# The attention mask moved from VectorE to GpSimd, the value copies from ScalarE to VectorE, and a layer norm folded into two fused operations

## The chip, the cores and the metric

The kernel runs on one core of a Trainium2 chip. The metric is the device time of one launch in microseconds. Before the change it took 445.38 us (median of three runs, 444.36 to 445.75).

The engines are named as in the profile: PE is TensorE (matrix products and transposes), DVE is VectorE, ACT is ScalarE, POOL is GpSimd, SP is SyncE, which here only issues DMAs. Each engine works through its own instruction queue in order and waits for the others by semaphores. SBUF is the on-chip memory, PSUM holds PE's results in eight banks.

## The reference, cut to what matters

Sixteen frames of 128 tokens by 128 channels pass through two decoder layers: cross attention to 120 context tokens with a feed-forward part, then a second cross attention with relative positions and another feed-forward part. The change touches the second attention and the layer norm behind it:

```python
attn = einsum('bidn,bjdn->bijn', hq, hk)                    # content scores, 16 heads
attn = attn + take_along_axis(b_full, idx, axis=2)          # relative position scores, shifted per row
attn = attn + ...                                           # the ub and vb terms
attn = attn / sqrt(128)
attn = where(attn_mask[..., None], -INF, attn)              # mask: 128 x 120 per frame, one for all heads
attn = softmax(attn, axis=2)
out  = einsum('bijn,bjdn->bidn', attn, hv)                  # hv: values of the context, 120 x 64 a head
out  = out * sigmoid(q @ head_w)
out  = out.reshape(...) @ Wo + residual
out  = (out - mean) / sqrt(var + 1e-5) * ln_g + ln_b
```

The result of this norm is added to the running frame x. In the inputs the mask is all false, but it is read and applied.

## The kernel before, in words

Everything is fp32. There are three stages, each a software pipeline over frames: the first attention (to about 126 us), the first feed-forward part (to about 170 us), and a third stage, `layer1(s, par)`, that does the second attention and its feed-forward part together. The change is only in the third stage.

In step s of the third stage different frames t are at different depths: frame s has its queries, keys and position products made, frame s-1 its content scores, frame s-2 its maxima and exponentials, frame s-3 and s-4 their scaling, transposes, value products and output, frame s-4 its norm, frames s-5 to s-7 the quantised feed-forward part. The order on every engine is written out by hand in `layer1`; buffers come in pairs, chosen by `p`. The 16 heads stand in four groups of four; group g of `prob[p]` is 128 x 480 (4 heads x 120 keys). The first steps, with few frames in flight, are the ramp here, the last ones, with no new frames, the drain. Steps 10 and 11 form a loop that runs once; all others are unrolled.

The relative shift is done through DRAM. PE makes unshifted position products; ACT copies them to `relw` (L567 to L627); SP stores them to `rel_scratch` and loads them back with a row stride one short (`store`, `shifted`, L255 to L266) into `relr[p]`. Half 1 (groups 2 and 3, semaphore `relr1`) is loaded at the end of step t, half 0 (groups 0 and 1, `relr0`) at the start of step t+1. DVE adds the content scores from PSUM to `relr` and writes `prob` (L1017, L1019, L1023 and, in the next step, L862; semaphores `added2`, `added3`, `added1`, `added0`). Each such addition also frees a PSUM bank that PE waits for.

Before the change DVE then applied the mask to each sum: `cap` is 0 where masked and 3e38 elsewhere, and `min(cap - 1e9, sum)` is taken, four operations of 128 x 480 a frame (L886, L897, L905, L1044; semaphore `masked`). The maxima (L874, L967, L969, L988) waited for `masked`. ACT takes the exponentials with their sums (L530), DVE the reciprocals (`rsum`, L1039 and L914), and POOL multiplies the probabilities by them (`scale_probs`, L383: groups 1 and 0 after the first `rsum` of the step, groups 3 and 2 after the second). PE transposes the scaled probabilities in two blocks (`probs_transpose`, L1262: first groups 0 and 1, then 2 and 3), ACT copies them out (`probT`), PE multiplies them with `hv`.

The values `hv` come from two PE products of 120 x 512, and ACT copied both from PSUM to SBUF (L563 and L602; `hv1` and `hv0` free the banks 0 and 6).

The norm of frame s-4: DVE takes mean and variance of `uo`, POOL the reciprocal root (L409), DVE `(uo - mean) * rstd` (L998), POOL multiplies by `ln_g` (L411), waits behind a spacer (L413) and adds `xb` = x + `ln_b` into `x_all` (L415; semaphore `x_done`, for which DVE's statistics of the next norm wait at L854).

## Time and profile before

The profiled execution took 446.94 us, its span (first to last instruction) 445.1 us; the rest lies around the span.

| engine | busy us | share of the span | instructions |
|---|---|---|---|
| PE, products | 413.2 | 93% | 6147 |
| PE, weight loads (beside the products) | 313.6 | 70% | 6147 |
| DVE | 374.7 | 84% | 1230 |
| ACT | 376.3 | 85% | 1478 |
| POOL | 250.2 | 56% | 364 |

The mean granted TensorE clock was 0.982 of full speed. Busy shares are means over all stages. The chain of work that ended last lies for 74% on PE, 12% on DVE, 6% on ACT. A column "idle before" in a view is the time in which the engine stood before an instruction, with the engine and line that ended the wait.

### The profile page before, as it was taken

The page shows a single profiled execution, that of the slowest core. Times are in us where ns is not written, and L with a number is a line of the kernel's source. Part 1 is how long each engine was busy: PE and PEld are TensorE (multiplying, and loading weights), DVE is VectorE, ACT ScalarE, POOL GpSimd, SP SyncE. Part 2 cuts the span into 40 slices and gives each one's busy share as a digit, 9 for nine tenths or more (in the row PEclk, how much of TensorE's full clock was granted, in tenths as well). Part 3 has the DMA queues.
Part 4 walks back from the last instruction along what each step waited for, and adds up shares of the span by engine and source line. Part 5 has one row for each costly group of instructions (what it writes and reads, how often), then busy time and mean ns, then how long its engine had stood idle before and what let it go on. Part 6 is the DMA issues. An engine that isn't in the chain of part 4 may idle for free.

```text
span 445.1 us, 16726 instructions
## 1 busy us (share of the span) xinstructions
PE 413.2 (93%) x6147; PEld 313.6 (70%) x6147; DVE 374.7 (84%) x1230; ACT 376.3 (85%) x1478; POOL 250.2 (56%) x364
## 2 busy tenths in 40 slices
PE   7999999999789997999999999999999999998782
PEld 6555565555456776877888888887878878887570
DVE  5799999989768884597788889888889978989865
ACT  1899999998955555599999999999999999999861
POOL 4297888878866651023346345554644654456654
PEclk9999999999989999999999999999999999999887
DMA  7251000000000002998766668567657856854000
GB/s 204 72 183 38 15 9 11 11 8 9 7 1 2 0 2 50 263 217 206 149 153 148 143 152 196 127 154 156 148 133 158 190 134 131 192 136 88 7 7 24
DMA packets 54392, 44.88 MB, mean 101 GB/s; under 512 B 43952, under 2 KB 49328, under 8 KB 54320
## 3 DMA queue, kind: packets, MB, share of 16 engines
q1 hardware_dynamic: 53616, 43.59, 40.9%
q8 instruction: 46, 0.75, 0.7%
q10 hardware_dynamic: 704, 0.32, 0.3%
q14 instruction: 26, 0.21, 0.2%
HBM read 22.92 MB, written 20.97 MB: 99 GB/s over the span
## 4 chain that ended last, share of the span: by engine, by line
PE 74%; DVE 12%; ACT 6%; POOL 2%; issue 2%; DMA 1%; SPq 1%; POOLq 0%; ACTq 0%; DVEq 0%
PE PS L1052 64%; PE PS L1262 4%; PE PS L1068 3%; ACT prob L530 2%; PE PS L1228 1%; DMA wr<-in_wr 1%; DVE nmax L715 1%; DVE nmax L717 1%; DVE relr L763 1%; POOL prob L326 1%; DVE relw L758 1%; DVE nmax L686 1%; PE PS L1218 1%; DVE probT L693 1%; DVE nmax L780 1%
## 5 line engine op out<-in xcount | busy, mean ns | idle before, releaser
L383 POOL TENSOR_TENSOR prob<-prob,rsum 128x480 f32<-128x480 f32 x63 | 65.4, 1059 | 88.7 <-DVE rsum L914 61.4
L530 ACT ACTIVATE prob<-prob,nmax 128x120 f32<-128x120 f32 x256 | 100.5, 426 | 0.0
L446 ACT ACTIVATE prob<-PS,nmax 128x120 f32<-128x120 f32 x256 | 89.6, 394 | 4.2 <-DVE nmax L780 2.5
L326 POOL TENSOR_TENSOR prob<-prob,rsum 128x480 f32<-128x480 f32 x64 | 62.5, 987 | 23.8 <-DVE rsum L753 12.7
L446 ACT ACTIVATION_READ_ACCUMULATOR prob<-PS,nmax 128x1 f32 x256 | 61.5, 240 | 0.0
L530 ACT ACTIVATION_READ_ACCUMULATOR prob<-prob,nmax 128x1 f32 x256 | 59.2, 231 | 0.0
L1052 PE MATMUL PS<-xnT,wq 128*128 128x128 f32 x288 | 43.1, 286 | 2.2 <-ACT xnT L599 1.1
L1052 PE MATMUL PS<-probT,hv 120*64 120x128 f32 x512 | 36.4, 286 | 5.3 <-ACT probT L617 3.2
L1052 PE MATMUL PS<-ctx,wk 128*128 128x120 f32 x288 | 41.1, 279 | 0.0
L1052 PE MATMUL PS<-rT,qv 64*32 64x152 f32 x2048 | 40.8, 292 | 0.3 <-DVE qu L881 0.3
L1052 PEld LDWEIGHTS PS<-probT,hv 120*64 120x64 f32 x512 | 28.4, 140 | 17.5 <-issue 7.7
L1052 PEld LDWEIGHTS PS<-xnT,wq 128*128 128x128 f32 x288 | 35.9, 191 | 5.2 <-issue 1.4
L1052 PE MATMUL PS<-wv,ctx 128*120 128x512 f32 (+1 forms) x96 | 39.1, 489 | 0.0
L1052 PE MATMUL PS<-wo,oT_pairs 128*128 128x128 f32 x256 | 36.2, 286 | 0.0
L1052 PEld LDWEIGHTS PS<-ctx,wk 128*128 128x128 f32 x288 | 36.0, 192 | 0.2 <-issue 0.2
L1052 PE MATMUL PS<-kT,qu 64*128 64x120 f32 x512 | 32.7, 276 | 2.3 <-issue 1.5
L1052 PE MATMUL PS<-relw,qT 32*128 32x480 f32 x128 | 34.4, 613 | 0.4 <-DVE relw L758 0.4
L1052 PEld LDWEIGHTS PS<-rT,qv 64*32 64x32 f32 x2048 | 31.0, 105 | 5.4 <-issue 4.0
L1052 PEld LDWEIGHTS PS<-wo,oT_pairs 128*128 128x128 f32 x256 | 31.8, 195 | 4.1 <-issue 4.0
L1052 PEld LDWEIGHTS PS<-kT,qu 64*128 64x128 f32 x512 | 30.3, 188 | 3.2 <-issue 1.8
L1068 PEld LDWEIGHTS PS<-ident,prob 64*120 64x120 f32 x512 | 18.1, 137 | 19.1 <-issue 19.1
L1068 PE MATMUL PS<-ident,prob 64*120 64x64 f32 x512 | 22.3, 228 | 5.4 <-POOL prob L326 2.9
(197 smaller groups left out, 1073.8 us busy)
## 6 DMA issues: line engine op xcount, KB each, us to landing
rel_scratch<-relw SPq DMA_DIRECT2D x128, 152.0 KB, 2.6
relr<-rel_scratch SPq DMA_DIRECT2D x64, 240.0 KB, 4.5
ctx<-in_ctxT SPq DMA_DIRECT2D x32, 60.0 KB, 1.9
out_x<-fin SPq DMA_DIRECT2D x16, 64.0 KB, 4.0
x_all<-in_x SPq DMA_DIRECT2D x1, 640.0 KB, 7.8
wr<-in_wr SPq DMA_DIRECT2D x1, 512.0 KB, 6.3
wq<-in_wq SPq DMA_DIRECT2D x1, 512.0 KB, 3.6
wk<-in_wk SPq DMA_DIRECT2D x1, 512.0 KB, 4.4
```

What stands on the lines that cost most here:

```text
L326: return pool.tensor_tensor(pr, pr, cols(rsum[p], g, HG).unsqueeze(2).to_broadcast([S, HG, SK]), ALU.mult)
L383: return pool.tensor_tensor(pr, pr, cols(rsum[p], g, HG).unsqueeze(2).to_broadcast([S, HG, SK]), ALU.mult)
L446: last = act.activation(cols(prob[p], n, SK), cols(scores, q, SK), ACT.Exp, bias=nmax[p][:, n:n + 1], accum_out=ssum[p][:, n:n + 1])
L530: last = act.activation(cols(pr, n, SK), cols(pr, n, SK), ACT.Exp, bias=bias[:, n:n + 1], accum_out=total[:, n:n + 1])
L686: dve.tensor_reduce(out=cols(nmax[p], 2, HG), in_=heads(PS[:, 3, 0:HG * SK], HG), op=ALU.max, axis=AX.X, negate=True).then_inc(A0["nmax"], 1)
L693: dve.tensor_copy(query_half(probT0[0], 1), heads(PS[0:SK, 6, :], 2 * HG)).then_inc(A0["probT1"], 1)
L715: dve.tensor_reduce(out=cols(nmax[p], 0, HG), in_=heads(PS[:, 0, 0:HG * SK], HG), op=ALU.max, axis=AX.X, negate=True).then_inc(A0["nmax"], 1)
L717: dve.tensor_reduce(out=cols(nmax[p], 1, HG), in_=heads(PS[:, 2, 0:HG * SK], HG), op=ALU.max, axis=AX.X, negate=True).then_inc(A0["nmax"], 1)
L758: dve.tensor_tensor(heads(kexp[p], HG), PS[:, 4, S:S + SK].unsqueeze(1).to_broadcast([D, HG, SK]), kmask_sb[:, :].unsqueeze(2).to_broadcas ...
L1052: return pe.matmul(o, a, b, start=start, stop=stop)
L1068: last = pe.transpose(PS[0:SK, bank, q * S // 2:(q + 1) * S // 2], cols(prob[p], g * HG + q, SK)[rows], ident_sb[rows, rows])
L1262: last = pe.transpose(PS[0:SK, bank, q * S // 2:(q + 1) * S // 2], cols(prob[p], g * HG + q, SK)[rows], ident_sb[rows, rows])
```

## The change

The four mask operations on DVE are gone. `cap` is now the mask times -1e30 (one operation as before, but at the start of DVE's step), and POOL adds it to the four groups of the reloaded position scores in `relr`, in place, before DVE adds the content scores. DVE's additions therefore wait for `masked` (two groups, then four) where they waited for `relr1` and `relr0`, and the maxima wait for the additions. On POOL the four additions stand between the two pairs of scalings. Both value copies move from ACT to DVE: `hv1` behind `qu0`, `hv0` behind the quantising. The norm becomes `(uo - mean) * ln_g` and `uo * rstd + xb`, two fused operations on DVE; POOL keeps the reciprocal root.

```diff
-BIG = 3.0e38
+NEG_MASK = -1.0e30
 ...
# POOL, layer1
+                def mask_scores(p, g):
+                    r = heads(cols(relr[p], g, HG * SK), HG)
+                    return pool.tensor_tensor(r, r, cap[p][:, :].unsqueeze(1).to_broadcast([S, HG, SK]), ALU.add)
                 t, p = s - 3, 1 - par
                 if on(t):
                     pool.wait_ge(A1["rsum"], 2 * t + 1)
                     scale_probs(p, 1).then_inc(A1["scaled1"], 1)
                     scale_probs(p, 0).then_inc(A1["scaled0"], 1)
+                t, p = s - 1, 1 - par
+                if on(t):
+                    pool.wait_ge(A1["cap"], t + 1)
+                    pool.wait_ge(A1[f"relr1{p}"], 2 * loads(t, p))
+                    mask_scores(p, 2).then_inc(A1["masked"], 1)
+                    mask_scores(p, 3).then_inc(A1["masked"], 1)
+                    pool.wait_ge(A1[f"relr0{p}"], 2 * loads(t, p))
+                    mask_scores(p, 1).then_inc(A1["masked"], 1)
+                    mask_scores(p, 0).then_inc(A1["masked"], 1)
+                t, p = s - 3, 1 - par
+                if on(t):
                     pool.wait_ge(A1["rsum"], 2 * t + 2)
                     scale_probs(p, 3).then_inc(A1["scaled3"], 1)
 ...
-                    pool.wait_ge(A1["onorm"], t + 1)
-                    pool.tensor_tensor(uo[p][:, :], uo[p][:, :], g_sb[:, :], ALU.mult).then_inc(A1["og"], 1)
-                    pool.wait_ge(A1["og"], t + 1)
-                    pool.tensor_tensor(gap_p[:, :], mhalf[:, :], mhalf[:, :], ALU.add)
-                    xt = x_all[:, bass.ds(t, 1), :].rearrange("p a d -> p (a d)")
-                    pool.tensor_tensor(xt, xb[p][:, :], uo[p][:, :], ALU.add).then_inc(A1["x_done"], 1)
# ACT, layer1
-                    act.wait_ge(A1["hv_ps"], 2 * t + 1)
-                    after(act, A1["av"], 4 * t - 4)
-                    act.activation(cols(hv[p], 1, 512), PS[0:SK, 0, :], ACT.Copy).then_inc(A1["hv1"], 1)
 ...
-                    act.activation(cols(hv[p], 0, 512), PS[0:SK, 6, :], ACT.Copy).then_inc(A1["hv0"], 1)
# DVE, layer1, at the start of the step
+                t, p = s - 1, 1 - par
+                if on(t):
+                    dve.wait_ge(A1[f"mask_loaded{p}"], loads(t, p))
+                    dve.tensor_scalar(cap[p][:, :], mask_sb[p][:, :], NEG_MASK, None, ALU.mult).then_inc(A1["cap"], 1)
 ...
-                    dve.wait_ge(A1["masked"], 4 * t + 1)
+                    dve.wait_ge(A1["added1"], t + 1)
 ...
-                    sc = heads(cols(prob[p], 3, HG * SK), HG)
-                    dve.scalar_tensor_tensor(out=sc, in0=cap[p][:, :].unsqueeze(1).to_broadcast([S, HG, SK]), scalar=NEG, in1=sc,
-                                             op0=ALU.add, op1=ALU.min).then_inc(A1["masked"], 1)
 ...
+                    dve.wait_ge(A1["hv_ps"], 2 * t + 1)
+                    after(dve, A1["av"], 4 * t - 4)
+                    dve.tensor_copy(cols(hv[p], 1, 512), PS[0:SK, 0, :]).then_inc(A1["hv1"], 1)
 ...
+                t, p = s - 2, par
+                if on(t):
+                    dve.wait_ge(A1["hv_ps"], 2 * t + 2)
+                    dve.tensor_copy(cols(hv[p], 0, 512), PS[0:SK, 6, :]).then_inc(A1["hv0"], 1)
 ...
                     dve.tensor_scalar(ve2[p][:, :], mv2[p][:, 1:2], 1e-5, None, ALU.add).then_inc(A1["ovar"], 1)
+                    dve.scalar_tensor_tensor(out=uo[p][:, :], in0=uo[p][:, :], scalar=mv2[p][:, 0:1], in1=g_sb[:, :],
+                                             op0=ALU.subtract, op1=ALU.mult).then_inc(A1["og"], 1)
 ...
-                    dve.tensor_scalar(uo[p][:, :], uo[p][:, :], mv2[p][:, 0:1], rstd2[p][:, :], ALU.subtract, ALU.mult)\
-                       .then_inc(A1["onorm"], 1)
+                    dve.wait_ge(A1["og"], t + 1)
+                    dve.wait_ge(A1["xb"], t + 1)
+                    dve.scalar_tensor_tensor(out=row(x_all, t), in0=uo[p][:, :], scalar=rstd2[p][:, :], in1=xb[p][:, :],
+                                             op0=ALU.mult, op1=ALU.add).then_inc(A1["x_done"], 1)
 ...
-                    dve.wait_ge(A1[f"relr1{p}"], 2 * loads(t, p))
+                    dve.wait_ge(A1["masked"], 4 * t + 2)
 ...
-                    dve.wait_ge(A1[f"relr0{p}"], 2 * loads(t, p))
+                    dve.wait_ge(A1["masked"], 4 * t + 4)
```

In the changed program POOL's queue at the ramp, up to step 3, reads as follows (before, then now). `rstd` is the reciprocal root for the norm of frame s+2, for which DVE's `xn` waits; `prob<-prob,rsum` are the scalings, `relr<-relr,cap` the mask additions.

```order
L419 TENSOR_TENSOR rstd<-ve,mhalf 128x1 x4
L425 TENSOR_TENSOR xb<-x_all,ln_b 128x128
L383 TENSOR_TENSOR prob<-prob,rsum 128x480 x4
L419 TENSOR_TENSOR rstd<-ve,mhalf 128x1
L425 TENSOR_TENSOR xb<-x_all,ln_b 128x128
```

```order
L428 TENSOR_TENSOR rstd<-ve,mhalf 128x1 x2
L387 TENSOR_TENSOR relr<-relr,cap 128x480 x4
L428 TENSOR_TENSOR rstd<-ve,mhalf 128x1
L387 TENSOR_TENSOR relr<-relr,cap 128x480 x4
L428 TENSOR_TENSOR rstd<-ve,mhalf 128x1
L434 TENSOR_TENSOR xb<-x_all,ln_b 128x128
L383 TENSOR_TENSOR prob<-prob,rsum 128x480 x2
L387 TENSOR_TENSOR relr<-relr,cap 128x480 x4
L383 TENSOR_TENSOR prob<-prob,rsum 128x480 x2
```

Four mask additions now stand ahead of `rstd` in steps 1 and 2, and between the pairs of scalings from step 3 on.

On DVE the same place, step 2 (frame 0 at its maxima), from `xn` at the end of step 1 to the second copy of the keys; `qu` are the query halves, `nmax` the maxima.

```order
L1031 TENSOR_SCALAR xn<-x_all,mv,rstd 128x128
L1044 SCALAR_TENSOR_TENSOR prob<-cap,prob 128x480
L862 TENSOR_TENSOR prob<-PS,relr 128x480
L869 TENSOR_SCALAR qu<-PS,ub 128x512
L874 TENSOR_REDUCE nmax<-prob 128x4
L881 TENSOR_SCALAR qu<-PS,ub 128x512
L886 SCALAR_TENSOR_TENSOR prob<-cap,prob 128x480
L892 TENSOR_SCALAR cap<-mask 128x120
L897 SCALAR_TENSOR_TENSOR prob<-cap,prob 128x480
L901 COPY xn_all<-xn 128x128
L905 SCALAR_TENSOR_TENSOR prob<-cap,prob 128x480
L952 COPY kT<-PS 128x480
```

```order
L1028 TENSOR_SCALAR xn<-x_all,mv,rstd 128x128
L864 TENSOR_SCALAR cap<-mask 128x120
L867 TENSOR_TENSOR prob<-PS,relr 128x480
L874 TENSOR_SCALAR qu<-PS,ub 128x512
L879 TENSOR_REDUCE nmax<-prob 128x4
L886 TENSOR_SCALAR qu<-PS,ub 128x512
L892 COPY hv<-PS 120x512
L895 COPY xn_all<-xn 128x128
L941 COPY hv<-PS 120x512
L945 COPY kT<-PS 128x480
```

The four mask operations have left, `cap` stands ahead of the last score addition, and the two value copies have come in, one directly behind the second `qu` and one ahead of the copy of the keys.

## Rows read from the trace of the kernel before

**Rows 1.** Busy time by stretch (start:end us, length; each engine; granted clock, DMA, GB/s).
```profile
260.00:400.00 140.00, 138.44 (x2513) 115.95 (x2511) 123.71 (x363) 135.16 (x489) 71.85 (x123) 1.00 0.66 152
120.00:128.00 8.00, 5.92 (x72) 3.91 (x72) 5.46 (x20) 5.69 (x20) 7.42 (x8) 0.79 0.01 3
```
**Rows 2.** Timeline of PE (start us, us, line, operation, count, idle before).
```profile
191.96 0.27 PE L1350 MATMUL PS<-ident,xn 128*128 128x128 f32 x1
...
208.08 0.69 PE L1262 MATMUL PS<-ident,prob 64*120 64x64 f32 x16
...
317.45 0.69 PE L1262 MATMUL PS<-ident,prob 64*120 64x64 f32 x16
...
321.78 1.06 PE L1052 MATMUL PS<-xnT,wq 128*128 128x128 f32 x8
...
407.67 1.09 PE L1052 MATMUL PS<-probT,hv 120*64 120x128 f32 x16 [1.18 <-ACT probT L617]
408.69 0.69 PE L1262 MATMUL PS<-ident,prob 64*120 64x64 f32 x16
```
**Rows 3.** Timeline of SP's queue: pairs of reload DMAs, frames 0, 2, 2, 9, 15.
```profile
179.38 1.34 SPq L266 DMA_DIRECT2D relr<-rel_scratch  x2
...
198.69 1.28 SPq L266 DMA_DIRECT2D relr<-rel_scratch  x2
...
200.23 1.25 SPq L266 DMA_DIRECT2D relr<-rel_scratch  x2
...
304.96 1.26 SPq L266 DMA_DIRECT2D relr<-rel_scratch  x2
...
400.37 1.25 SPq L266 DMA_DIRECT2D relr<-rel_scratch  x2
```
**Rows 4.** Tile relr in five windows: landing times of the pairs of rows 3.
```profile
DMA to landing us min/median/max: 4.2/4.6/4.9
...
DMA to landing us min/median/max: 3.7/4.7/5.6
...
DMA to landing us min/median/max: 4.9/5.3/5.7
...
DMA to landing us min/median/max: 4.7/5.0/5.3
...
DMA to landing us min/median/max: 4.1/4.9/5.6
```
**Rows 5.** Timeline of POOL: scaling of groups 3 and 2 in a middle step.
```profile
312.57 1.93 POOL L383 TENSOR_TENSOR prob<-prob,rsum 128x480 f32<-128x480 f32 x2 [4.33 <-DVE rsum L914]
```
**Rows 6.** Single lines: duration ns min/median/max, first and last start us.
```profile
L351 POOL TENSOR_TENSOR hsq<-hsq,wup x1: 1270/1270/1270, 97.4 to 97.4; 128x512 f32<-128x512 f32 x1
...
L383 POOL TENSOR_TENSOR prob<-prob,rsum x63: 982/987/1292, 198.7 to 428.1; 128x480 f32<-128x480 f32 x63
...
L922 DVE TENSOR_SCALAR qx<-xf x16: 227/960/962, 249.5 to 440.9; 128x128 f32<-128x128 f32 x16
...
L941 DVE COPY probT<-PS x1: 691/691/691, 428.0 to 428.0; 120x512 f32<-120x512 f32 x1
```
**Rows 7.** Timeline of DVE in step 2 and in a middle step.
```profile
187.50 0.34 DVE L1031 TENSOR_SCALAR xn<-x_all,mv,rstd 128x128 f32<-128x128 f32 x1
...
190.10 0.74 DVE L881 TENSOR_SCALAR qu<-PS,ub 128x512 f32<-128x512 f32 x1
...
319.70 0.65 DVE L1019 TENSOR_TENSOR prob<-PS,relr 128x480 f32<-128x480 f32 x1
```
**Rows 8.** Chain that ended last, in order of time (start us, us, what).
```profile
201.32 0.48 ACT hv L563
...
333.06 0.62 PE PS L1262 x14
...
436.64 0.50 POOL uo L411
...
437.40 0.41 POOL x_all L415
```

More of the change, by code:

```diff
@@ L884, in layer1 @@
                 if on(t):
-                    sc = heads(cols(prob[p], 3, HG * SK), HG)
-                    dve.scalar_tensor_tensor(out=sc, in0=cap[p][:, :].unsqueeze(1).to_broadcast([S, HG, SK]), scalar=NEG, in1=sc,
-                                             op0=ALU.add, op1=ALU.min).then_inc(A1["masked"], 1)
-                t, p = s - 1, 1 - par
-                if on(t):
-                    dve.wait_ge(A1[f"mask_loaded{p}"], loads(t, p))
-                    dve.wait_ge(A1[f"mask_loaded{p}"], loads(t, p))
-                    dve.tensor_scalar(cap[p][:, :], mask_sb[p][:, :], 1.0, -BIG, ALU.subtract, ALU.mult).then_inc(A1["cap"], 1)
-                t, p = s - 2, par
-                if on(t):
-                    dve.wait_ge(A1["added0"], t + 1)
-                    sc = heads(cols(prob[p], 0, HG * SK), HG)
-                    dve.scalar_tensor_tensor(out=sc, in0=cap[p][:, :].unsqueeze(1).to_broadcast([S, HG, SK]), scalar=NEG, in1=sc,
-                                             op0=ALU.add, op1=ALU.min).then_inc(A1["masked"], 1)
+                    dve.wait_ge(A1["hv_ps"], 2 * t + 1)
+                    after(dve, A1["av"], 4 * t - 4)
+                    dve.tensor_copy(cols(hv[p], 1, 512), PS[0:SK, 0, :]).then_inc(A1["hv1"], 1)
                 t, p = s, par
@@ L901, in layer1 @@
                     dve.tensor_copy(row(xn_all, t), xn[p][:, :]).then_inc(A1["xn_kept"], 1)
-                t, p = s - 2, par
-                if on(t):
-                    sc = heads(cols(prob[p], 2, HG * SK), HG)
-                    dve.scalar_tensor_tensor(out=sc, in0=cap[p][:, :].unsqueeze(1).to_broadcast([S, HG, SK]), scalar=NEG, in1=sc,
-                                             op0=ALU.add, op1=ALU.min).then_inc(A1["masked"], 1)
                 def denominators():
@@ L986, in layer1 @@
                 if on(t):
-                    dve.wait_ge(A1["masked"], 4 * t + 4)
+                    dve.wait_ge(A1["added2"], t + 1)
                     dve.tensor_reduce(out=cols(nmax[p], 2, HG), in_=heads(cols(prob[p], 2, HG * SK), HG), op=ALU.max, axis=AX.X,
@@ L1039, in layer1 @@
                     dve.reciprocal(cols(rsum[p], 0, 2 * HG), cols(rsum[p], 0, 2 * HG)).then_inc(A1["rsum"], 1)
-                t, p = s - 1, 1 - par
-                if on(t):
-                    dve.wait_ge(A1["added1"], t + 1)
-                    sc = heads(cols(prob[p], 1, HG * SK), HG)
-                    dve.scalar_tensor_tensor(out=sc, in0=cap[p][:, :].unsqueeze(1).to_broadcast([S, HG, SK]), scalar=NEG, in1=sc,
-                                             op0=ALU.add, op1=ALU.min).then_inc(A1["masked"], 1)
             run_steps(dve, attn0, ffn0, layer1, crossing)
```

8 lines of the change are left out of this document (2 added, 6 removed).

## The prediction, written before the changed kernel ran

> **What bounds the kernel now.** I read the engine totals first: four engines above half busy, PE highest. Totals mix stages, so next the busy time by stretch [rows 1]: from 260 to 400 us, nine steps of the third stage, PE is busy 138.4 of 140 us at full granted clock, ACT 135.2, DVE 123.7, POOL 71.9. The chain of waits says the same: between 208 and 406 us it is almost only PE pieces, one period from the next as 317.5 and 333.1 are for the same block [rows 2, 8]. So inside the stage no relief of ACT or DVE can give more than the 1.6 us in which PE was idle. What can move the end is a new wait that reaches PE, anywhere, since PE has no slack to make it good, and the ramp (up to 208 us) and the drain (from 406), where the chain runs through ACT, DVE and POOL. The last view is therefore the timeline of PE where it meets this change [rows 2], beside SP's loads and their landings [rows 3, 4] and POOL [rows 5].
>
> **The moved wait, the heart of it.** A POOL step used to be: scale groups 1 and 0 of frame s-3, scale 3 and 2, then small work. Now the four mask additions of frame s-1 stand between the two pairs, and the last two of them wait for the second half of the reloaded position scores, which SP issues at the start of the same step. Scaling 3 and 2 is queued behind that wait, and PE's second block of transposes waits for that scaling.
>
> Prices. Mask addition: 128x480, two full streams from SBUF. Above: the 128x512 operation on POOL took 1.270 us, by size 1.19 for 480. Below: the scaling of the same shape, whose second input is one value per head, 0.98 [rows 6]. I take 1.2, since the mask is walked element by element, as in the nearer row. A pair of scalings takes 1.93 [rows 5].
> On this price the Trainium skill, page GPSIMD Engine Reference, section 3.1, gives 4497 ns for 2048 fp32 elements of a two-input add; by size that is an estimate of 1.05 us for 480, between my ends, and by it the sum would be about 0.9 us lower (six mask additions lie on the path).
>
> *Ramp, frame 0.* The first half of its reload has landed at 179.38 + 0.65 + 4.9 = 184.9 (the second DMA of a pair is issued some 0.65 after the first) [rows 3, 4]. Four masks end at 189.7, and the reciprocal root of a later frame's norm, about 0.5 us of POOL, is queued behind them. DVE waits for it with xn, which starts at 190.2 instead of 187.50. From there to the end of qu0 it took 3.3 us [rows 7]; the first of the two value copies comes on top (0.69 by the same shape [rows 6]), less the mask that leaves. PE's transpose of xn, which needs the bank that this copy frees, stood at 191.96 [rows 2] and comes at about 193.8: 1.8 late.
>
> *Ramp, step 3, frame 2.* First half landed: 198.69 + 0.65 + 5.6 = 204.9; second: 200.23 + 0.65 + 5.7 = 206.6 [rows 3, 4]. Two masks to 207.3, two more to 209.7, scaling 3 and 2 to 211.6. Before, PE's block ran at 208.08 [rows 2]: 3.5 us late with loads at their old times. They now come later too, because the relw copies that feed them are behind the 1.8 us above; ACT's missing value copies (0.48 each [rows 8]) give 0.5 back, and I estimate that SP's own backlog of stores hides 0.3 more: +1.0. Ramp together **+4.5**. Ends: +1.6 (masks at 0.98, landing after 4.9, nothing passed on), and +6.
>
> *Clock.* PE then stands about 4 us with nothing to do. In the stretch 120 to 128 us, where PE ran with gaps and was busy 5.9 of 8 us, the mean granted clock was 0.79 [rows 1]: 1.7 us of full-speed work lost. Ends: 0, and 3.4 (a second such stretch in the drain). I take **+1.7**, because only dense PE work follows this wait.
>
> *Inside.* Typical step: second half landed 304.96 + 0.65 + 5.3 = 310.9 [rows 3, 4]; masks to 313.3, scaling to 315.2, where POOL started it at 312.57 before [rows 5]; PE's block stands at 317.45 [rows 2]. 2.2 us of cover, less in a step whose loads land late. POOL's own load: 71.9 us over nine steps is 8.0, less 1.1 (uo, spacer, x_all), plus 4.8: 11.7 of 15.5, it fits. DVE loses four masks and gains two copies and one small operation, ACT loses 1.0: both gains are hidden by PE. The fused norm stands in the later half of DVE's step and delays the score additions by about 0.3: the one at 319.70 ended 1.4 us before PE's next use of its bank at 321.78 [rows 2, 7]. Take **+0.2** (0 to 3).
>
> *Drain, step 16.* This step is short, since PE has no new frame. Second half of frame 15: 400.37 + 0.65 + 5.6 = 406.6; masks to 409.0, scaling to 410.9, against PE's block at 408.69 [rows 2 to 4]: 2.2 late. ACT copies the transposes next and is itself the chain from there; its two value copies are gone before the next block, worth 0.8 where PE follows close behind. Net **+1.4** (-0.5 to +2.5).
>
> *Tail.* On the chain after the last norm stood POOL uo and x_all, 0.50 and 0.41 with a spacer of 0.2 between [rows 8]. One DVE operation of some 0.35 replaces them, but the queues around keep part: **-0.6** (-1 to 0).
>
> Sum: 4.5 + 1.7 + 0.2 + 1.4 - 0.6 = +7.2. The profiled execution took 446.94 us itself (span 445.1), so it would be 454.1; the median of the runs is 445.38, 1.6 below it, and the forecast for the median is **452.6**.
>
> **A rule that bears on it.** DVE's quantising operation (L922) took 0.960 us at the median and 0.227 at its shortest; POOL's scaling took 1.292 at most against 0.982 [rows 6]. Each is long where the other engine is at work in SBUF. The Trainium skill, page SBUF — State Buffer, section "SBUF: two separate sides", calls the port pair that DVE and GpSimd share an exclusive lock held for the whole instruction. The rows agree; the rule speaks against filling POOL's idle time, and what it would do here is the third rival.
>
> **Rivals.**
> 1. *The ramp's wait without the lowered clock.* For it: PE was idle 1.18 us before 407.67 and its next products took their usual time [rows 2]. Against: this wait is three times that. 452.6 - 1.7 = 450.9.
> 2. *The relief wins (faster).* Place: the ramp, where three of ACT's value copies lie on the chain between 190 and 207 us, the drain and the tail. Price: -1.5 - 0.8 - 0.6 = -2.9, so 442.5. It decides if the reloads land early enough: masks and scaling end 4.3 us after the landing, so in step 3 it would have to come by 203.8, and the trace has 206.6.
> 3. *DVE late in every step.* With POOL masking through most of DVE's first half, cap, the copy of xn and the first quantising operation can each wait up to 0.73 us (0.960 - 0.227) more: 2.2 a step, less 0.5 by which ACT now releases DVE earlier, plus 0.3 for the fused norm, is 2.0 against the cover of 1.4. 0.6 us a step over 11 steps adds 6.6: 459.2. Against: DVE idles before the denominators and absorbs the first two.
> 4. *Ends cancel (same).* Landings near 4 us and masks at 0.98 make the ramp +1.6, the drain -0.5, the tail -0.6: +0.5, so 445.9.
>
> **How the numbers follow.** The measurement tells 0.3% (1.3 us) from no change. Chances: forecast 0.54, rival 1 0.20, rival 3 0.10 (all slower: 0.84); rival 4 0.10 (same), rival 2 0.06 (faster). The range runs from between rivals 4 and 1 to just under rival 3: 447.0 to 457.5. That leaves out rivals 2 and 4 below and most of rival 3 above, about 0.2 together.
>
> **What would show it.** In step 3 the chain should pass from PE to POOL (masks, then scaling) and back, with about 4 us of PE idle near 209 to 213 us, POOL waiting for the landing of relr before a mask, and a granted clock below 1 right after. Wrong if scaling 3 and 2 of step 3 ends before PE has finished its value products. From 260 to 400 us a step should still be 15.5 us; if it is longer, rival 3 holds and PE waits for added2 or added3 of DVE. ACT should show 32 fewer copies and waits in their place. In the tail the last norm should end some 0.6 sooner. The forecast is wrong as a whole if the time is under 447, which means that the ramp hid the landing.

## The result, and the profile after

| | before | after |
|---|---|---|
| median of the runs made side by side, us | 444.87 (443.82 to 445.75, 4 runs) | 468.13 (467.05 to 468.67, 4 runs) |
| ratio, 95% interval | | 1.051 (1.046 to 1.056) |
| profiled execution, us | 446.94 | 468.51 |
| its span, us | 445.1 | 466.7 |
| busy share PE / DVE / ACT / POOL | 93 / 84 / 85 / 56% | 89 / 83 / 78 / 65% |

The change costs 23 us; 7 had been forecast. The direction was right and the size was not: the time lies above the whole range. Ratios and their intervals here leave out single slow executions, such as one of 514.92 us among the ten of e4 (granted clock 0.749). First, the stretches of [rows 1], and the clock behind the ramp.

The changed kernel, busy time by stretch (columns as in rows 1):
```profile
214.00:216.00 2.00, 0.66 (x12) 0.69 (x14) 0.00 (x0) 0.00 (x0) 2.00 (x4) 0.78 1.01 215
216.00:218.00 2.00, 2.00 (x25) 2.00 (x24) 0.00 (x0) 1.51 (x5) 0.02 (x1) 0.50 1.14 212
218.00:220.00 2.00, 2.00 (x26) 1.89 (x23) 1.71 (x4) 1.83 (x10) 0.00 (x0) 0.87 0.36 63
260.00:400.00 140.00, 127.69 (x2294) 107.30 (x2301) 124.06 (x334) 116.23 (x429) 95.71 (x123) 0.99 0.61 141
382.00:386.00 4.00, 4.00 (x94) 3.21 (x80) 3.74 (x17) 2.65 (x9) 3.23 (x8) 0.57 0.21 48
432.70:460.00 27.30, 19.91 (x252) 15.79 (x252) 23.43 (x82) 19.18 (x73) 17.28 (x32) 1.00 0.04 11
```
The kernel before, in its drain:
```profile
418.00:426.00 8.00, 6.47 (x56) 5.40 (x57) 5.73 (x22) 6.71 (x28) 6.27 (x12) 0.57 0.03 8
```
The last two rows of the first view and the one of the second matter later: both kernels have stretches of lowered clock, but in different places. Now look at the row from 260 to 400: PE is busy 127.7 us where it was 138.4. That is the stretch in which the forecast saw nothing happen. The wait list of that stretch names one line of PE, nine times (L1043 is the line of a helper that many blocks share; by PE's timeline all nine stand before the same block, the position products):
```profile
PE PS L1043 <- issue: 12.3, 9, 1.8
```
"issue" means that the view found nothing that PE waited for. The timelines of PE and DVE over one step tell what it was. PE of the changed kernel: steps 3 and 5, one middle step, drain (answers to rows 2):
```profile
215.34 1.11 PE L1253 MATMUL PS<-ident,prob 64*120 64x64 f32 x16 [4.95 <-POOL prob L383]
...
247.99 0.68 PE L1253 MATMUL PS<-ident,prob 64*120 64x64 f32 x16 [0.36 <-POOL prob L383]
...
330.33 1.27 PE L1043 MATMUL PS<-rT,qv 64*32 64x152 f32 x64 [1.66 <-issue]
332.56 0.68 PE L1253 MATMUL PS<-ident,prob 64*120 64x64 f32 x16
...
432.64 0.69 PE L1253 MATMUL PS<-ident,prob 64*120 64x64 f32 x16 [1.42 <-POOL prob L383]
```
DVE of the changed kernel ahead of that block:
```profile
325.51 0.98 DVE L900 SCALAR_TENSOR_TENSOR rsum<-ez,ssum 128x8 f32<-128x8 f32 x1 [1.64 <-ACT prob L539]
326.52 0.20 DVE L903 RECIPROCAL rsum<-rsum 128x8 f32<-128x8 f32 x1
326.64 1.07 DVE L909 TENSOR_SCALAR xf<-xf,tiny 128x128 f32<-128x128 f32 x1
327.74 1.13 DVE L911 TENSOR_SCALAR qx<-xf 128x128 f32<-128x128 f32 x1
328.79 0.68 DVE L941 COPY hv<-PS 120x512 f32<-120x512 f32 x1
329.39 0.64 DVE L945 COPY kT<-PS 128x480 f32<-128x480 f32 x1
329.96 0.28 DVE L917 TENSOR_TENSOR uo<-PS,xn_all 128x128 f32<-128x128 f32 x1
```
POOL of the changed kernel, ramp and the same step (answers to rows 5):
```profile
185.63 4.68 POOL L387 TENSOR_TENSOR relr<-relr,cap 128x480 f32<-128x480 f32 x4 [9.85 <-DMA relr<-rel_scratch]
190.27 0.55 POOL L428 TENSOR_TENSOR rstd<-ve,mhalf 128x1 f32<-128x1 f32 x1
...
208.52 4.68 POOL L387 TENSOR_TENSOR relr<-relr,cap 128x480 f32<-128x480 f32 x4 [5.21 <-DMA relr<-rel_scratch]
213.15 1.94 POOL L383 TENSOR_TENSOR prob<-prob,rsum 128x480 f32<-128x480 f32 x2
...
324.10 4.68 POOL L387 TENSOR_TENSOR relr<-relr,cap 128x480 f32<-128x480 f32 x4 [2.53 <-DMA relr<-rel_scratch]
328.75 1.92 POOL L383 TENSOR_TENSOR prob<-prob,rsum 128x480 f32<-128x480 f32 x2
```
Lay the last two fences beside each other. POOL's four additions run from 324.10, one every 1.17 us, so they end near 325.30, 326.47, 327.64 and 328.78. DVE's denominators operation on 128x8 elements begins at 325.51 and ends at 326.49; the next small operation ends at 327.71, the quantising one at 328.87. Each ends within 0.1 us behind an addition of POOL. The residual addition (L917) comes last in this row of work. It reads y from PSUM bank 2, and PE's block of position products (rT, qv) needs that bank: the residual ends at 330.24, PE starts at 330.33. In the kernel before, DVE stood idle ahead of the residual, waiting for y, and was done before PE came (DVE, then PE):
```profile
330.21 0.29 DVE L928 TENSOR_TENSOR uo<-PS,xn_all 128x128 f32<-128x128 f32 x1 [0.24 <-PE PS L1052]
```
```profile
330.71 1.27 PE L1052 MATMUL PS<-rT,qv 64*32 64x152 f32 x64
```

The same operations over the whole run (duration ns min/median/max). In the kernel before, the medians of the first two of DVE were 168 and 236; the quantising one stood at 960 [rows 6] and has 911 now:
```profile
L387 POOL TENSOR_TENSOR relr<-relr,cap x64: 1195/1206/1223, 185.6 to 429.3; 128x480 f32<-128x480 f32 x64
...
L900 DVE SCALAR_TENSOR_TENSOR rsum<-ez,ssum x16: 159/822/1187, 205.7 to 449.5; 128x8 f32<-128x8 f32 x16
...
L909 DVE TENSOR_SCALAR xf<-xf,tiny x16: 235/1066/1077, 258.4 to 462.1; 128x128 f32<-128x128 f32 x16
...
L941 DVE COPY hv<-PS x16: 640/678/692, 194.6 to 441.5; 120x512 f32<-120x512 f32 x16
```
The chain that ended last shows the ramp and the drain (answers to rows 8):
```profile
202.46 5.92 DMA relr<-rel_scratch
...
208.52 4.68 POOL relr L387 x4
213.20 1.90 POOL prob L383 x2
...
421.06 4.61 DMA relr<-rel_scratch
425.80 4.69 POOL relr L387 x4
430.49 1.89 POOL prob L383 x2
```
Both times all four additions follow one landing without a gap. It is the landing of the first half (in step 3 at 208.39); the second half, landed at 209.85, was there before its two additions came up.

Three marks in PE's timeline cut the stage so that kernels can be compared: PE's first transpose of xn in this stage (near 167 us), the second transposes of step 3 (before 208.08) and those of step 16 (before 408.69), and the end of the span. The first mark itself lies between 165.5 and 169.1 us in these profiles, ahead of the stage that was changed, so the pieces after it tell more than the spans. All from one profiled execution each, us:

| kernel | ratio of times (95%) | ramp | steps 3 to 16 | tail |
|---|---|---|---|---|
| before | 1 | 41.1 | 200.6 | 36.4 |
| after | 1.051 (1.046, 1.056) | 48.4 | 217.3 | 34.1 |
| masks only (e1) | 1.036 (1.028, 1.044) | 47.8 | 212.1 | 34.9 |
| value copies only (e2) | 1.003 (0.999, 1.007) | 41.3 | 199.6 | 37.2 |
| norm only (e3) | 0.991 (0.987, 0.994) | 41.1 | 198.4 | 34.2 |
| full, POOL doesn't mask (e4) | 0.992 (0.988, 0.995) | 40.6 | 200.1 | 33.5 |
| full, residual first (e5) | 1.026 (1.018, 1.034) | 46.1 | 207.8 | 34.0 |
| full, masks behind (e6) | 1.011 (1.004, 1.017) | 43.3 | 201.0 | 35.4 |
| e6, residual first (e7) | 1.030 (1.024, 1.035) | 43.1 | 210.9 | 37.1 |
| e6, value copies on ACT (e8) | 1.009 (1.006, 1.012) | 43.0 | 202.2 | 35.6 |
| additions nobody waits for (e9) | 1.045 (1.037, 1.053) | 47.3 | 215.7 | 35.0 |
| the same without waits (e10) | 1.005 (1.001, 1.009) | 40.6 | 204.8 | 34.1 |
| sets in their place (e11) | 1.021 (1.010, 1.032) | 47.4 | 203.9 | 35.1 |
| before, with values and norm moved (e12) | 1.003 (1.000, 1.006) | 41.2 | 199.2 | 36.4 |

From before to after: ramp +7.2, steps +16.7, tail -2.3, together the 21.6 us of the two spans. The pieces hold lowered clock too. PE's clock was granted at half, for 3.2 us behind the second mark and 3.4 us near 384, in the steps of the changed kernel, which is 3.3 us of full-speed work; in the tail before (418 to 426 us: 0.57) it is 3.4 us, where the changed kernel has none up to 460.

### The profile page after: what moved, and what is told of

Same layout as the page of the kernel before. It is cut to its first block, busy times and chain, and to the rows that moved or that the text cites. A ratio compares the mean times of both kernels' runs of the same rounds, so it can differ in the third digit from the quotient of the medians.

```text
span 466.7 us, 16710 instructions
## 1 busy us (share of the span) xinstructions
PE 415.6 (89%) x6147; PEld 315.1 (68%) x6147; DVE 385.1 (83%) x1214; ACT 362.2 (78%) x1446; POOL 304.5 (65%) x380
## 4 chain that ended last, share of the span: by engine, by line
PE 59%; DVE 14%; POOL 8%; DMA 7%; issue 5%; SPq 3%; ACT 3%; POOLq 0%; DVEq 0%; ACTq 0%
PE PS L1043 50%; DMA relr<-rel_scratch 5%; POOL relr L387 4%; PE PS L1253 3%; PE PS L1059 3%; SPq L258 2%; PE PS L1219 1%; DMA rel_scratch<-relw 1%; DMA wr<-in_wr 1%; POOL prob L383 1%; DVE relr L764 1%; DVE nmax L716 1%; DVE nmax L718 1%; POOL prob L326 1%; DVE relw L759 1%
## 5 line engine op out<-in xcount | busy, mean ns | idle before, releaser
L539 ACT ACTIVATE prob<-prob,nmax 128x120 f32<-128x120 f32 x256 | 99.4, 410 | 2.0 <-DVE nmax L960 1.7
L387 POOL TENSOR_TENSOR relr<-relr,cap 128x480 f32<-128x480 f32 x64 | 75.3, 1206 | 39.1 <-DMA relr<-rel_scratch 38.8
L383 POOL TENSOR_TENSOR prob<-prob,rsum 128x480 f32<-128x480 f32 x63 | 60.9, 989 | 45.6 <-DVE rsum L1036 43.2
L326 POOL TENSOR_TENSOR prob<-prob,rsum 128x480 f32<-128x480 f32 x64 | 62.5, 987 | 22.8 <-DVE rsum L754 12.7
L539 ACT ACTIVATION_READ_ACCUMULATOR prob<-prob,nmax 128x1 f32 x256 | 55.3, 216 | 0.0
L1043 PE MATMUL PS<-rT,qv 64*32 64x152 f32 x2048 | 41.3, 295 | 14.8 <-issue 13.7
L1043 PE MATMUL PS<-xnT,wq 128*128 128x128 f32 x288 | 43.2, 286 | 3.5 <-DVE prob L1016 1.3
L1043 PEld LDWEIGHTS PS<-rT,qv 64*32 64x32 f32 x2048 | 31.5, 106 | 20.4 <-issue 19.7
L1043 PE MATMUL PS<-ctx,wk 128*128 128x120 f32 x288 | 41.1, 279 | 0.0
L1043 PEld LDWEIGHTS PS<-xnT,wq 128*128 128x128 f32 x288 | 35.9, 191 | 6.6 <-DVE prob L1016 1.4
L1043 PE MATMUL PS<-probT,hv 120*64 120x128 f32 x512 | 35.9, 284 | 4.7 <-ACT probT L618 2.4
L1043 PE MATMUL PS<-wv,ctx 128*120 128x512 f32 (+1 forms) x96 | 39.1, 489 | 0.0
L1043 PEld LDWEIGHTS PS<-probT,hv 120*64 120x64 f32 x512 | 28.0, 139 | 16.2 <-issue 9.8
L1043 PEld LDWEIGHTS PS<-ctx,wk 128*128 128x128 f32 x288 | 36.0, 192 | 0.2
L1043 PE MATMUL PS<-wo,oT_pairs 128*128 128x128 f32 x256 | 35.6, 282 | 0.0
L1043 PE MATMUL PS<-relw,qT 32*128 32x480 f32 x128 | 34.4, 613 | 0.4 <-DVE relw L759 0.4
L1043 PE MATMUL PS<-kT,qu 64*128 64x120 f32 x512 | 33.4, 281 | 0.7 <-ACT relw L624 0.7
L1043 PEld LDWEIGHTS PS<-wo,oT_pairs 128*128 128x128 f32 x256 | 31.1, 191 | 3.9 <-issue 3.6
L1043 PEld LDWEIGHTS PS<-kT,qu 64*128 64x128 f32 x512 | 31.2, 194 | 1.4 <-ACT relw L624 1.4
```

The costliest lines, as they stand in the source:

```text
L326: return pool.tensor_tensor(pr, pr, cols(rsum[p], g, HG).unsqueeze(2).to_broadcast([S, HG, SK]), ALU.mult)
L383: return pool.tensor_tensor(pr, pr, cols(rsum[p], g, HG).unsqueeze(2).to_broadcast([S, HG, SK]), ALU.mult)
L387: return pool.tensor_tensor(r, r, cap[p][:, :].unsqueeze(1).to_broadcast([S, HG, SK]), ALU.add)
L539: last = act.activation(cols(pr, n, SK), cols(pr, n, SK), ACT.Exp, bias=bias[:, n:n + 1], accum_out=total[:, n:n + 1])
L1043: return pe.matmul(o, a, b, start=start, stop=stop)
```

## Experiments

**Theory T** from the traces: POOL's additions hold DVE's small operations up, and with the value copy ahead of it the residual addition comes too late for PE's bank 2. Rivals: **R**, the landing of the reload and the scaling behind it; **V**, the value copies on DVE; later **M**, DVE's wait for the masks. Each kernel was run side by side with the kernel before.

### e1_masks_only: the first part alone

```
 the full change, but:
+ act:  hv1 and hv0 copies as before    - dve: hv1 and hv0 copies
+ pool: uo, spacer, x_all as before     - dve: the two fused norm operations
```


> The mask move alone: value copies on ACT and the norm as before. Theory T (DVE's residual addition, which frees PSUM bank 2 for the third block of position products, is late because POOL's masks hold up DVE's small SBUF operations by 1.8 us and the value copy hv0 stands ahead of it by 0.6): the wait of PE before those products falls from 1.6 to about 1.0 us a step, the ramp keeps its stall of some 5 us and one stretch at half clock, total about 461. Rival R (the middle steps are long because the scaling of groups 3 and 2 waits for the landings of relr): as in the full change, 468, with the wait before the second transposes. Rival V (the value copies on DVE are the cause): about 452, only the ramp's loss.

462.27 us against 446.15 of before, ratio 1.036. The first part alone makes about 16 of the 23 us. PE waits for "issue" ten times, 6.8 us between 260 and 400; eight of these waits, 6.2 us, stand before the position products. R and V are both off by over 5 us. T stands.

### e2_values_only: the value copies alone

```
 the kernel before, but:
- act.activation(cols(hv[p], 1, 512), PS[0:SK, 0, :], ACT.Copy)   (and the same for hv0, bank 6)
+ dve.tensor_copy(cols(hv[p], 1, 512), PS[0:SK, 0, :])            (behind qu0; hv0 ahead of kT0)
```


> Only the two value copies moved from ACT to DVE, masks on DVE and norm as before. T: DVE has 0.24 us of cover before the residual addition, so 0.6 more makes PE wait 0.2 to 0.4 us a step (2 to 4 us in all), ACT's relief gives 1.5 back in the ramp: 445 to 448. V: PE waits 1.5 us a step, 460. R: no change, 443 to 445.

447.83 us, ratio 1.003 (0.999 to 1.007): no difference that these runs can tell. The time is in T's range, but the wait of 0.2 to 0.4 us a step that T expected is not there: PE waits once, 0.9 us, between 260 and 400. V falls: the copy ahead of the residual harms nobody while the operations before it are short.

### e4_after_unmasked: the change without the additions

```
 the full change, but:
- pool: mask_scores(p, 2), (p, 3), (p, 1), (p, 0) and their waits
  dve: waits for relr itself before the score additions (the mask is not applied)
```


> The full change with the four mask additions on POOL left out altogether (no mask is applied; DVE waits for the reloads directly), value copies on DVE and fused norm kept. T: L900 falls from 0.95 to 0.17 us and L909 from 1.07 to 0.24, PE's wait in the middle steps to under 0.3 us, no stall in the ramp: 443 to 446. V: middle steps stay at 17 us, 460. R: 443 to 446 as well, but then with DVE's small operations unchanged in length.

442.7 us, ratio 0.992, just under T's range. The change without POOL's additions, so with no mask at all, is a gain of 0.8%. Against this kernel the additions cost 1.051/0.992, or 6%, some 26 us. The small operations are short again (ns min/median/max), yet the quantising one is not, since it still meets a scaling:
```profile
L894 DVE SCALAR_TENSOR_TENSOR rsum<-ez,ssum x16: 166/168/169, 204.4 to 425.4; 128x8 f32<-128x8 f32 x16
...
L903 DVE TENSOR_SCALAR xf<-xf,tiny x16: 234/236/990, 250.6 to 438.0; 128x128 f32<-128x128 f32 x16
...
L905 DVE TENSOR_SCALAR qx<-xf x16: 227/1026/1028, 250.9 to 438.3; 128x128 f32<-128x128 f32 x16
```

### e5_residual_first: the order on DVE

```
 the full change, but (dve, middle steps):
+ residual()
  hv0 copy; kT0 copy
- residual()
```


> The full change with one move on DVE: the residual addition (semaphore u, frees PSUM bank 2) stands ahead of the value copy hv0 and the key copy kT0 instead of behind them; the work is the same. T: it comes 1.2 us earlier, PE's wait before the third block of position products falls from 1.6 to about 0.5 us, 10 steps: 468 - 11 = 457. If that wait is for something else (qu0, relw2, an instruction fetch, the landings of relr) nothing changes: 468.

456.87 us, ratio 1.026: 11 us of the 23 are gone with the additions untouched. In the steps it is 217.3 to 207.8, of which the lowered clock near 384, absent here, makes 1.7. PE's waits before the position products are nearly gone. It now waits at another block, the output products (wo), for the copy of qu0, which the late DVE reaches later (PE waits, 260 to 400; L1043 is again the shared line):
```profile
PE PS L1043 <- DVE qu L886: 2.5, 7, 0.4
PE PS L1043 <- issue: 0.7, 2, 0.4
```
That the operations are slow and that they stand ahead of the residual are two halves of one cause: e4 takes away the one, e5 part of the other.

### e6_masks_behind: the additions behind POOL's other work

```
 pool, full change:                    pool, e6:
 scale 1, 0                            scale 1, 0; scale 3, 2
 masks 2, 3, 1, 0 (wait for relr)      fin, rstd_f, mask 2, rstd_o, mask 3, rstd
 scale 3, 2; fin, roots; xb            masks 1, 0; xb
```


> The full change; only POOL's order differs: the four mask additions stand behind POOL's scalings and, in pieces, between and behind its reciprocal roots, and the last two position scores are waited for one by one. Theory T (the mask additions cost through two things only: they hold POOL's scalings back at the ramp and in the drain, and they stretch the small VectorE operations that stand ahead of the residual addition and so hold TensorE's position products): both go, the value copy ahead of the residual addition stays. So the second transposes of step 3 come near 209 again, TensorE's busy time between 260 and 400 is above 137 us, small denominators operations fall back to 0.17 to 0.24 us; 444 to 449 us, ratio 1.00 +- 0.007. Rival Q (POOL's queue: the mask additions now come late for the score additions on VectorE, and what they meet there is stretched as much): TensorE waits in each step for another of VectorE's operations, 130 us busy between 260 and 400, 455 to 462 us. Rival L (VectorE and POOL together simply have too much work): 460 us or more wherever the masks stand.

450.18 us, ratio 1.011 (1.004 to 1.017). Moving the same 64 additions takes back 18 of 23 us; Q and L are both wrong. The ratio is a little above what T gave: the ramp stays 2 us longer, and DVE operations are stretched here too, only where there is more room. From DVE's timeline of this kernel, three operations that take 0.34, 0.16 and 0.22 us in the kernel with the norm alone. The first runs under a mask addition, the second under POOL's addition for `xb`, the third under a scaling:
```profile
322.89 0.64 DVE L1002 SCALAR_TENSOR_TENSOR x_all<-uo,rstd_o,xb 128x128 f32<-128x128 f32 x1
...
326.38 0.42 DVE L1040 SCALAR_TENSOR_TENSOR rsum<-ez,ssum 128x8 f32<-128x8 f32 x1
...
327.53 0.66 DVE L870 TENSOR_SCALAR cap<-mask 128x120 f32<-128x120 uint8 x1
```

### e7_behind_residual: both cures at once

```
 e6, but (dve, middle steps): residual() ahead of the hv0 and kT0 copies, as in e5
```


> As e6_masks_behind, and besides VectorE adds the residual ahead of the value copy of bank 6 and of kT0. Theory T: takes the 0.6 us of the copy out of the residual's way too, a further 0 to 4 us off e6: 441 to 447 us. Rival Q: as e6, 455 to 462, for what is late is not the residual.

459.18 us, ratio 1.030: a miss of 12 us, and the wrong sign against e6. DVE's timeline of this kernel shows why:
```profile
321.14 0.29 DVE L924 TENSOR_TENSOR uo<-PS,xn_all 128x128 f32<-128x128 f32 x1 [1.47 <-PE PS L1050]
321.35 0.68 DVE L950 COPY hv<-PS 120x512 f32<-120x512 f32 x1
```
Once DVE is on time, y is not there yet when it comes to the residual. It stands still for 1.47 us with two copies queued behind, and these, then qu0, come late: PE waits for qu0 eight times between 260 and 400, 3.0 us in all. The order that gained 11 us with DVE late loses 9 us with DVE in time. T was right on the mechanism in the changed kernel and too simple on what follows when it is gone.

### e8_behind_values_act: e6 with the value copies back on ACT

```
 e6, but: act copies hv1 and hv0, as before
```


> As e6_masks_behind, with both value copies back on ScalarE. Theory T: VectorE is relieved by 4 mask operations and pays 2 copies less, 441 to 447 us, equal to e7 within 3 us. If the value copies on VectorE cost nothing by themselves (as in the run with the copies alone), e8 equals e6 within 2 us. Rival Q: 455 to 462.

448.61 us, ratio 1.009, equal to e6 within its interval and 1.6 us above T's range. It doesn't equal e7, which had failed for its own reason. No cost of the value copies can be told here either.

### e3_norm_only: the third part alone

```
 the kernel before, but:
- dve: uo = (uo - mean) * rstd    - pool: uo = uo * g; spacer; x_all = xb + uo
+ dve: uo = (uo - mean) * g       + dve: x_all = uo * rstd + xb
```


> The kernel before with the output norm in two fused VectorE operations alone. My prediction's term for it: 0.6 us off the tail, nothing inside: 443 to 446 us, ratio 0.995 to 1.001. Rival N (the second fused operation, which waits for POOL's root and xb, holds VectorE's queue in every step): 450 us or more.

442.03 us, ratio 0.991 (0.987 to 0.994), 0.4% below the lower end expected. Only this one and e4 beat both kernels with their intervals, and e4 leaves the mask out, so this is the one to keep. Part of the gain goes with the granted clock, 0.984 at the median of the runs against 0.979: among the runs at 0.983 and 0.984 this kernel took 441.15 to 443.10 us (five), the one before 442.73 to 444.11 (four), 1.4 us apart by medians. The chain of its tail goes from the root straight on, where before DVE's and POOL's operations for uo and x_all stood between:
```profile
430.14 0.56 POOL rstd_o L409
430.70 0.43 POOL fin L397
```
Before, from the start of that root (435.66) to the start of the second fin (437.81) it took 2.15 us; now 0.56. That is 1.6 us here; the tail is shorter by 2.3, but the tail before also holds the lowered clock from 418 to 426 us, and this one is at full clock to 431.

### e9_idle_additions, e10_additions_no_wait, e11_idle_sets: what it is in an addition

```
 e4, but in pool where the masks stood:
 e9:   wait relr1; scr2 += ln_g; scr3 += ln_g; wait relr0; scr1 += ln_g; scr0 += ln_g
 e10:  the same four additions, no wait for relr
 e11:  wait relr1; set 2, 3 (128x1200) to zero; wait relr0; set 1, 0
 (scr: scratch buffers of 128x480 that nobody reads; the mask is not applied)
```


> The full change, but POOL's four additions of a step, in the same place, of the same size and behind the same waits for the reload, go into a scratch buffer that nobody waits for (mask not applied; VectorE waits for the reload itself). Theory T (the steps are longer since POOL's additions, while they run, stretch VectorE's operations ahead of the residual): the steps stay near 17 us, TensorE is busy about 128 us between 260 and 400, the denominators operation takes 0.5 to 1.1 us; 464 to 469 us. Rival M (VectorE's wait for the mask additions is what costs): steps fall to 15.6 us, about 450 to 455 us with what the ramp still costs.

> As e9_idle_additions, but POOL does not wait for the reload either: the additions start right behind the scalings of groups 1 and 0 (mask not applied). Theory T: at the ramp and in the drain POOL's second scalings are late by 4.8 us at most and not by a landing besides, so the ramp's and the drain's loss halves or goes; in the steps the additions still lie over the denominators, perhaps a little earlier: 452 to 464 us, steps 16 to 17 us. Rival M: 443 to 447 us, as without the additions.

> As e9_idle_additions, but in place of each addition POOL sets a scratch buffer of 128x1200 to zero, an operation that reads nothing (its time is not known from the traces; if it is near 1 us POOL is busy as long as with the additions; mask not applied). Theory T in its narrow form (what VectorE waits for is POOL's reading of two SBUF operands): the denominators operation falls to 0.17 to 0.3 us and the steps to 15.6, 446 to 456 us by what the ramp costs. Rival B (any POOL operation of that length does it, or POOL's queue holding back its scalings does): steps stay at 17, 460 us or more.

e9: 466.09 us, ratio 1.045; the intervals of e9 and of the full change overlap. Additions whose result nobody uses cost nearly as much as the masks, so M falls: what is left for DVE's wait is 0.6% by the medians. The timelines of e9, POOL first, then DVE:
```profile
321.85 2.37 POOL L403 TENSOR_TENSOR scratch<-scratch,ln_g 128x480 f32<-128x480 f32 x2 [2.45 <-DMA relr<-rel_scratch]
324.17 2.37 POOL L407 TENSOR_TENSOR scratch<-scratch,ln_g 128x480 f32<-128x480 f32 x2
```
```profile
323.37 0.87 DVE L905 SCALAR_TENSOR_TENSOR rsum<-ez,ssum 128x8 f32<-128x8 f32 x1 [1.66 <-ACT prob L544]
324.39 1.06 DVE L914 TENSOR_SCALAR xf<-xf,tiny 128x128 f32<-128x128 f32 x1
```
e11: 456.89 us, ratio 1.021. A set took 1.10 us at the median (1.097 to 1.188), so POOL is busy about as long as with the additions, and its waits are the same. POOL, and DVE under it:
```profile
319.87 2.14 POOL L405 MEMSET scratch<- 128x1200 f32 x2 [0.59 <-DMA relr<-rel_scratch]
```
```profile
320.89 0.17 DVE L903 SCALAR_TENSOR_TENSOR rsum<-ez,ssum 128x8 f32<-128x8 f32 x1 [1.37 <-ACT prob L542]
```
```profile
L903 DVE SCALAR_TENSOR_TENSOR rsum<-ez,ssum x16: 166/167/168, 208.5 to 437.5; 128x8 f32<-128x8 f32 x16
...
L914 DVE TENSOR_SCALAR qx<-xf x16: 226/1080/1082, 258.8 to 450.4; 128x128 f32<-128x128 f32 x16
```
The denominators operation runs from 320.89 to 321.06, across the boundary of two sets, and takes 0.17 us; twelve of its sixteen executions lie under a set, and all take 0.166 to 0.168. For this operation it is not enough that POOL is busy: the additions, which read SBUF, hold it up, and the sets, which only write (and are another kind of operation), don't. That isn't so for all of DVE's small operations. The quantising one still takes 1.08 us at the median under the sets, and the copy of xn, 0.21 us by itself, took 2.13 at 224.99, across two sets. So a set still holds up those two, and what e11 takes away is one wait for POOL in the row ahead of the residual: from the start of the denominators to the start of the residual it is 3.24 us here and 4.34 in e9.

The steps fall from 215.7 (e9) to 203.9 us, and PE's ten waits before the position products, 13.0 us in e9, are gone but for one of 0.46; ramp and tail stay. So e9 and e11 part the loss. By profiles:

- **ramp 6.8 us** (40.6 to 47.4): POOL's queue behind the landing. The sums are alike in e9 and e11, the parts are not: in e9 PE waits 2.2 us for a score addition in step 2 and 4.1 for the scaling in step 3, in e11 2.4 and 2.4 with lowered clock between (0.50 from 196 to 198).
- **3.8** between steps 3 and 16 (200.1 to 203.9): 2.2 a wait for the scaling at step 16, most of the rest the lowered clock behind the ramp's wait (0.50 from 216 to 218).
- **11.8** that goes when POOL's operations no longer read (203.9 to 215.7).
- **1.6** from e9 to the full change (215.7 to 217.3). This isn't shown to be the waits for the masks: the lowered clock near 384, worth 1.7, is in the profile of the full change and not in that of e9.

By ratios of medians against e4 it is 2.9% from e4 to e11, 2.4% on to e9 and 0.6% on to the full change, or 13, 11 and 3 us. e11 itself came out 0.9 us above T's range, and its four runs spread from 451.8 to 457.6.

The Trainium skill, page SBUF — State Buffer, section "SBUF: two separate sides", says that a VectorE operation with two SBUF inputs contends only with a GpSimd operation that reads SBUF, and that whoever starts second waits for the whole instruction of the other. For the denominators operation, which has two SBUF inputs, e9 against e11 is that sentence as an experiment, and the ends of DVE's operations just behind the ends of POOL's show the second half. The trace agrees with both.

e10: 447.34 us, ratio 1.005. Both forecasts missed, T (452 to 464) by 5 us and M by 0.3: starting earlier helped far more than T had thought. Without the wait for the landing the same additions cost no ramp at all (40.6) and a third of the step loss (204.8 against 200.1 in e4; PE is busy 135.4 of 140 us): they begin sooner, and in the row ahead of the residual only the denominators operation still meets one, the last. What made the four additions dear is when they run, and they run then because they wait for a load in the middle of POOL's queue.

### e12_without_masks: the second and third part together

```
 the kernel before with e2 and e3
```


> The kernel before with the second and third part of the change (value copies on VectorE, norm in two fused operations), the masks as before. If the parts add up (norm alone 0.991, value copies alone 1.003 of the kernel before), the ratio is 0.994 +- 0.004, about 442 to 444 us. Rival (VectorE has too little room for both: in the kernel before it is busy 124 of 140 us between 260 and 400, and the copies bring it to 134): VectorE becomes late in every step, TensorE waits there, 448 us or more.

446.24 us, ratio 1.003 (1.000 to 1.006). Neither forecast holds: on top of the norm alone the value copies cost 1.2%. Against e4, nearly the same kernel with no mask at all, DVE's four mask operations cost 1.1% (1.003 against 0.992), where POOL's additions cost 6% in the middle of its queue. It isn't the rival: no wait of PE is listed from 260 to 400, where PE is busy 139.5 of 140 us. But the gain of the norm is gone: its tail is 36.4 us, where the norm alone has 34.2. In the drain PE waits 0.86 us for POOL's scaling and 1.70 for the copies of the last probabilities, where the norm alone has no such wait and 0.92. In its DVE timeline a value copy (415.79, 0.68 us) stands between the maxima and the denominators of a drain step, where PE no longer hides it; e2 has the same wait of 0.86 us, e4 has not. That this is the whole of it no run tests, and the profiles don't say so: of the 6.3 us between the spans of e12 and e3 3.2 lie ahead of the first mark, and e12 has 3.4 us of lowered clock from 425 that e3 has not.

## Why the prediction was wrong

**The step that failed is "Inside", +0.2 us with an upper end of 3.** Between the marks of steps 3 and 16 the stage grew by 16.7 us; "Inside", "Clock" and "Drain" together had put 3.3 there. By the changed kernel's profile PE waits ten times before the position products, 13.7 us in all, where the kernel before has two waits of 1.5 in all at another block. Waits for the scaling are 0.36 (step 5) and 1.42 (step 16), and lowered clock makes 3.3. These parts add up to 17.3, near the 16.7. So some 12 us stand where "Inside" had 0.2. The step's own sum held (landing, masks, scaling: in the step shown the scaling ends at 330.67 and PE's transposes stand at 332.56, so that cover was there). What it left out was how DVE and PE meet. Three errors in it:

- It took as DVE's cover the 1.4 us of one score addition [rows 2, 7]. It did not look for the tightest meeting of DVE and PE. That was the residual and bank 2: in the timeline of the kernel before it ran from 330.21 to 330.50, behind 0.24 us of idle time, and PE's block stood at 330.71. The room there was 0.24 + 0.21 us at most.
- It charged the two value copies to DVE's load and not to their place. hv0 (0.68) stands ahead of the residual. Alone that costs nothing (e2): idle time further ahead, 0.59 us before the denominators in the step shown, takes it up. Behind late operations it adds (e5, which moves it and the copy of the keys away, gains 11 us).
- Rival 3 had the mechanism, the lock between POOL and DVE, but priced only three operations by the one pair in the trace (0.960 and 0.227), let DVE's idle time "absorb the first two", and named added2 and added3 as the place. The operation directly behind that idle time, the denominators one, was itself held up, 0.17 to 0.82 at the median, and so was the next small one, 0.24 to 1.07: idle time ahead of an operation absorbs nothing of what happens to it. With its chance of 0.10 and 459.2 us it was the nearest case and still 9 us short.

**Ramp, step 3: right in kind, too small.** PE's block came at 215.34 instead of 208.08, 7.3 late against 4.5, above the end of 6 (the 1.7 for the clock falls behind this mark). The wait of 4.95 us lay where it was said. The path was not quite the one named: I let the landing of the second half and two masks decide, and in the trace it is the landing of the first half and all four masks. By my own numbers both give 211.6, so this was luck and cost nothing. The mis-sized term is the +1.0 by which the loads come later. The first half was issued at 201.82 instead of 198.69, 3.1 later, and landed at 208.39 instead of 204.9, 3.5 later.

**Clock: right behind the wait, not the whole of it.** Granted clock 0.78, 0.50 and 0.87 in the three stretches behind the wait: 0.44 + 1.00 + 0.26 is 1.7 us of full-speed work, as forecast; 0.50 is the lower of the two levels, and PE had stood 4.95 us before it. What wasn't forecast: a second such stretch (0.57 from 382 to 386, 1.7 us more), behind PE's longest wait before the position products (1.81 us), and that the one in the drain before (0.57 from 418 to 426, 3.4 us) is gone. Over the whole run the mean granted clock is 0.982 before and 0.979 after, so little of it is left as a net loss.

**Mask price: right.** 1.206 us against 1.2 taken. By the estimate from the figure of the Trainium skill (GPSIMD Engine Reference, section 3.1), 1.05, the six additions that I counted would be 0.9 us shorter; the measurement decides for the nearest row of the trace.

**Drain: right by luck.** PE waits 1.42 us and +1.4 had been forecast. But again the path is the first half's landing (425.67) and four masks, to 430.49, then the scaling to 432.38.

**Tail: right sign, too small.** -2.3 against -0.6. I had kept most of the removed work in the queues around it; e3 shows that POOL's next operation follows its root at once, 1.6 us. How the 2.3 divide is open: e1, with the norm as before, also has a shorter tail (34.9), and the lowered clock of the drain is in the tail before and not in the one after.

**Relief (rival 2): not where it was looked for.** Its largest price was 1.5 us in the ramp for ACT's copies. With the value copies alone (e2) the ramp is 41.3 us, as before, and in e4 it is 0.5 shorter. The gains of e3 and e4, 0.9 and 0.8%, come with the norm and in part with the clock; that of e4 was hidden under 26 us of additions.

## What to carry to other kernels

Before work goes to an idle POOL, list what DVE runs under it. A DVE operation of the kinds stretched here (two SBUF inputs, or one with scalars or a copy from SBUF tile to SBUF tile) can become as long as POOL's operation, however small it is: 0.17 us became up to 1.19. One such operation per step is enough when a bank of PE hangs behind it. Look for the tightest meeting between the two engines in the trace, not for a typical one, and count everything queued ahead of it. And look twice before work that waits for a load goes into the middle of an engine's queue: the same additions cost 6% there and 2% behind it (1.051 and 1.011 over 0.992). Test an order anew after every other change: the same move gained 11 us with DVE late and lost 9 with DVE on time. Last, look where the granted clock is low in each profile before you compare pieces of two of them.

## What was not expected of the hardware

- A 128x8 operation of DVE (0.168 us) took up to 1.187 us under POOL's additions of 1.206 us, and 0.167 us under sets of 1.10 us that read nothing.
- Sets that only write still held up other small operations: the quantising one, 0.23 us at its shortest, took 1.08 at the median in e11, and the copy of xn, 0.21 at its shortest, took up to 2.13, behind two sets in a row.
- Under the additions DVE's operations from PSUM and its reductions kept their time: the value copy 0.678 (0.691 for its shape before), reductions 0.64 in both kernels. POOL's additions too varied little (1.195 to 1.223), so in this case it was DVE that waited, nearly always.
